# A gated linear-attention and ternary-FFN layer: the mean square of the gated output is built from squares on GpSimd, one transpose and a VectorE sum

## The reference, cut to what matters

```python
x = L0_attn_hidden_states                      # [16, 512, 256]
xn = _layernorm(x, axis=-1)
x = x + _L0_attn_ref(xn, ...) + _L0_ffn_ref(xn, ...)
...
# the end of the attention part
o = gla_chunk_scan(q * SCALE, kn, v, rt_log)
o = o + shift * residual_weight
xg = o * jax.nn.silu(final_gate)               # [B, T, 512]
rms = jax.lax.rsqrt(jnp.mean(xg * xg, axis=-1, keepdims=True) + NORM_EPS)
o = xg * rms * norm_weight
return o @ down_w.T
...
# the FFN part: three layers of width 1024
h = jax.nn.silu(_tlin(x, w1_w, w1_s)) * _tlin(x, w2_w, w2_s)
h = jax.nn.gelu(_tlin(h, h1_w, h1_s), approximate=False)
h = jax.nn.gelu(_tlin(h, h2_w, h2_s), approximate=False)
return _tlin(h, w3_w, w3_s)
```

## Time and profile before

| What | Value |
|---|---|
| Time before, median of 3 runs | 1962.21 us (1960.61 to 1963.9) |
| Time of the profiled execution | 1961.79 us |
| Its span, first to last instruction | 1960.0 us |
| Granted TensorE clock, mean | 0.999 |
| PE busy | 1941.9 us, 99% |
| DVE busy | 1581.3 us, 81% |
| ACT busy | 1266.1 us, 65% |
| POOL busy | 68.4 us, 3% |

### The profile page before, as it was taken

One profiled execution on the slowest core, in us unless ns is written; L12 is line 12 of the kernel. 1 busy time (PEld: TensorE's weight loads), 2 busy tenths in 40 slices (PEclk: granted clock), 3 DMA queues, 4 the chain that ended last, 5 costly groups with the idle time before them and its releaser, 6 DMA issues.

```text
span 1960.0 us, 46467 instructions
## 1 busy us (share of the span) xinstructions
PE 1941.9 (99%) x17284; PEld 1928.9 (98%) x17284; DVE 1581.3 (81%) x4271; ACT 1266.1 (65%) x2527; POOL 68.4 (3%) x104
## 2 busy tenths in 40 slices
PE   8999999999999999999999999999999999999998
PEld 7999999999999999999999999999999999999998
DVE  7787878878788887887878788787888878878777
ACT  5675656766566766666656566666666666667564
POOL 0000000000000000000000000000000000000000
PEclk9999999999999999999999999999999999999999
DMA  8000000000000000000000000000000000000000
GB/s 309 7 12 12 12 7 6 12 12 12 12 1 12 12 12 12 12 1 12 12 12 12 11 2 12 12 12 12 1 12 12 12 12 12 2 12 12 13 7 8
DMA packets 23538, 34.38 MB, mean 18 GB/s; under 512 B 3042, under 2 KB 19810, under 8 KB 23364
## 3 DMA queue, kind: packets, MB, share of 16 engines
q1 hardware_dynamic: 23364, 31.63, 4.9%
HBM read 23.24 MB, written 8.39 MB: 16 GB/s over the span
## 4 chain that ended last, share of the span: by engine, by line
PE 93%; issue 3%; DVE 2%; ACT 1%; SPq 1%; DMA 0%; POOLq 0%; POOL 0%; DVEq 0%; ACTq 0%
PE fb L364 63%; PE ab L364 20%; PE ab L569 2%; PE ab L602 1%; PE ab L510 1%; PE ab L434 1%; PE ab L499 1%; PE fb L650 1%; SPq L272 0%; PE ab L562 0%; PE ab L450 0%; PE ab L581 0%; PE ab L561 0%; DVE hid0l L941 0%; ACT raw L806 0%
## 5 line engine op out<-in xcount | busy, mean ns | idle before, releaser
L364 PE MATMUL fb<-hid1h,wwhole 128*128 128x256 f32 x2048 | 475.4, 280 | 1.2 <-DVE hid1l L862 1.2
L364 PE MATMUL fb<-hid1l,wwhole 128*128 128x256 f32 x2048 | 468.9, 276 | 0.0
L364 PE MATMUL fb<-hid0l,wwhole 128*128 128x256 f32 x2048 | 466.4, 276 | 0.0
L364 PE MATMUL fb<-hid0h,wwhole 128*128 128x256 f32 x2048 | 466.4, 276 | 0.0
L364 PEld LDWEIGHTS fb<-hid1h,wwhole 128*128 128x128 f32 x2048 | 384.5, 188 | 4.0 <-ACT hid1h L721 0.9
L364 PEld LDWEIGHTS fb<-hid1l,wwhole 128*128 128x128 f32 x2048 | 384.7, 188 | 0.0
L364 PEld LDWEIGHTS fb<-hid0l,wwhole 128*128 128x128 f32 x2048 | 384.5, 188 | 0.0
L364 PEld LDWEIGHTS fb<-hid0h,wwhole 128*128 128x128 f32 x2048 | 384.5, 188 | 0.0
L806 ACT ACTIVATE raw<-fb,sh_s 128x256 f32<-128x256 f32 x512 | 212.8, 467 | 128.3 <-PE fb L364 126.2
L364 PE MATMUL fb<-xntl,wwhole 128*128 128x256 f32 x1024 | 237.5, 276 | 0.0
L364 PE MATMUL fb<-xnth,wwhole 128*128 128x256 f32 x1024 | 237.5, 276 | 0.0
(11 more groups left out here) (217 smaller groups left out, 4483.2 us busy)
## 6 DMA issues: line engine op xcount, KB each, us to landing
xin<-x SPq DMA_DIRECT2D x32, 256.0 KB, 2.7
out<-xin SPq DMA_DIRECT2D x32, 256.0 KB, 2.2
stage_more<-stage_w SPq DMA_DIRECT2D x6, 512.0 KB, 7.3
sgate<-stage_w SPq DMA_DIRECT2D x4, 512.0 KB, 5.1
shift<-stage_w SPq DMA_DIRECT2D x4, 512.0 KB, 5.6
v<-stage_w SPq DMA_DIRECT2D x4, 512.0 KB, 5.7
raw<-stage_w SPq DMA_DIRECT2D x3, 512.0 KB, 6.1
mixed<-stage_w SPq DMA_DIRECT2D x3, 512.0 KB, 8.4
```

Source lines behind the costliest of these rows:

```text
L364: mm = pe.matmul(o, a, b, start=start and i == 0, stop=stop and i == len(pairs) - 1)
```

## The change

The squares leave ACT. POOL multiplies `sgate` by itself in four instructions per half, one for each pair of a chunk `c` and a block of 64 channel rows `r`: the result lies on the 64 partitions `rows(c)` of `sq`. `sq` is now [128, 8, 128], with chunk 0 on partitions 0 to 63 and chunk 1 on 64 to 127. DVE sums the eight blocks into `sqsum` [128, 128]. PE transposes `sqsum` in one pass, so that tokens lie on the partitions, and DVE sums the 64 columns of each chunk (`total`, [128, 2]) before it scales them to `msq`. In the profile's rows of a changed kernel the lines are a few numbers higher than in the kernel before.

```diff
--- before.py
+++ after.py
@@ -163,9 +163,9 @@
         tanhv = work[:, 0:NC * DI].rearrange("p (c d) -> p c d", c=NC)
         lev = work[:, 0:LEVELS * CH].rearrange("p (l t) -> p l t", l=LEVELS)
         levq = work[:, LEVELS * CH:LEVELS * (CH + UP)].rearrange("p (l t) -> p l t", l=LEVELS)
-        sq = work[:, 0:DB * N].rearrange("p (d t) -> p d t", d=DB)
+        sq = work[:, 0:NC * DB * CH].rearrange("p (d t) -> p d t", d=NC * DB)
         xn = work[:, DB * N:DB * N + NC * H].rearrange("p (c h) -> p c h", c=NC)
-        sqsum = work[:, DB * N + NC * H:]
+        sqsum = work[:, DB * N + NC * H:DB * N + NC * H + CH]
         att = sb("att", [P, NC, CH])
         atth, attl = sb("atth", [P, 2, CH], F32R), sb("attl", [P, 2, CH], F32R)
         stateh, statel = sb("stateh", [P, DI], F32R), sb("statel", [P, DI], F32R)
@@ -179,6 +179,7 @@
         msq, rms = sb("msq", [P, NC]), sb("rms", [P, NC])
         nbt, later_k, earlier_q = sb("nbt", [P, 1]), sb("later_k", [P, 1]), sb("earlier_q", [P, 1])
         qk_sum = sb("qk_sum", [P, NC])
+        total = sb("total", [P, NC])
 
         fb = [ctx.enter_context(nc.psum_tensor(f"fb{i}", [P, 512], F32)) for i in range(4)]
         ab = [ctx.enter_context(nc.psum_tensor(f"ab{i}", [P, 512], F32)) for i in range(4)]
@@ -207,7 +208,7 @@
         kd_hi, st_hi, q_hi = seq_sig("kd_hi", NC), seq_sig("st_hi", 1), seq_sig("q_hi", 1)
         st_copy, st_sum = seq_sig("st_copy", 1), seq_sig("st_sum", 1)
         gelu1_d, hid1_hi, gelu2_d, hid2_hi = sig("gelu1_d", FB), sig("hid1_hi", 4), sig("gelu2_d", FB), sig("hid2_hi", 4)
-        sq_d, xg_hi, ln_hi = sig("sq_d", 1), sig("xg_hi", 1), sig("ln_hi", 1, 1)
+        sq_d, xg_hi, ln_hi = sig("sq_d", NC * NC), sig("xg_hi", 1), sig("ln_hi", 1, 1)
 
         conv_d, l1_d, hid0_lo, shift_lo = sig("conv_d", DB * (W - 1)), sig("l1_d", FB), sig("hid0_lo", 4), sig("shift_lo", 1)
         z_lo = sig("z_lo", 1)
@@ -220,7 +221,7 @@
         qs_d, q_lo = seq_sig("qs_d", 1), seq_sig("q_lo", 1)
         ss_d, att_d, mask_d = sig("ss_d", 1), sig("att_d", LEVELS + 2), sig("mask_d", NC)
         o_d, xg_d, xg_lo = sig("o_d", 2, 2), sig("xg_d", 1), sig("xg_lo", 1)
-        sqsum_d = sig("sqsum_d", 1)
+        sqsum_d, total_d = sig("sqsum_d", 1), sig("total_d", 1)
         hid1_lo, hid2_lo = sig("hid1_lo", 4), sig("hid2_lo", 4)
         msq_d, fin_d, stat_d, var_d, xn_d, ln_lo = (sig("msq_d", 1, 1), sig("fin_d", 5, 5), sig("stat_d", 3, 3),
                                                     sig("var_d", 1, 1), sig("xn_d", 1, 1), sig("ln_lo", 1, 1))
@@ -345,6 +346,11 @@
                 pool.tensor_tensor(rkn[:], ssk[:], minus_half[:], ALU.pow).then_inc(rkn_d.sem, 1)
                 if not (last and p == HALVES - 1):
                     normalise(me)
+                pool.wait_ge(xg_d.sem, xg_d.at(me))
+                for c in range(NC):
+                    for r in range(NC):
+                        part = sgate[rows(r), :, c * CH:(c + 1) * CH]
+                        pool.tensor_tensor(sq[rows(c), r * DB:(r + 1) * DB, :], part, part, ALU.mult).then_inc(sq_d.sem, 1)
                 pool.wait_ge(msq_d.sem, msq_d.at(me))
                 pool.tensor_tensor(rms[:], msq[:], minus_half[:], ALU.pow).then_inc(rms_d.sem, 1)
 
@@ -646,9 +652,7 @@
                 mm.then_inc(dn_mm.sem, 1)
                 pe.wait_ge(sqsum_d.sem, sqsum_d.at(me))
                 pe.wait_ge(gelu2_d.sem, gelu2_d.at(me, 4))
-                for c in range(NC):
-                    mm = pe.matmul(fb[1][:, c:c + 1], sqsum[:, c * CH:(c + 1) * CH], ones[:, 0:1], start=True, stop=True)
-                mm.then_inc(rs_mm.sem, 1)
+                pe.transpose(fb[1][:, 0:P], sqsum, ident_s[:]).then_inc(rs_mm.sem, 1)
 
             def sequences(exact):
                 with rounds(pe) as seq:
@@ -837,7 +841,6 @@
                 if not (last and p == HALVES - 1):
                     ln_high(me)
 
-                act.activation(sq[:], sgate[:], ACT.Square).then_inc(sq_d.sem, 1)
                 if p == 0:
                     act.wait_ge(st_sum.sem, st_sum.at(seq))
                     act.activation(stateh[rows(0), :], state, ACT.Copy)
@@ -1176,7 +1179,10 @@
                     low(statel[rows(0), :], state, stateh[rows(0), :])
                     low(statel[rows(1), :], state, stateh[rows(0), :]).then_inc(st_lo.sem, 1)
                 dve.wait_ge(rs_mm.sem, rs_mm.at(me))
-                dve.tensor_scalar(msq[:], fb[1][:, 0:NC], 1.0 / DI, EPS, ALU.mult, ALU.add).then_inc(msq_d.sem, 1)
+                dve.tensor_reduce(total[:], fb[1][:, 0:P].rearrange("p (c k) -> p c k", c=NC), mybir.AxisListType.X,
+                                  ALU.add).then_inc(total_d.sem, 1)
+                dve.wait_ge(total_d.sem, total_d.at(me))
+                dve.tensor_scalar(msq[:], total[:], 1.0 / DI, EPS, ALU.mult, ALU.add).then_inc(msq_d.sem, 1)
                 dve.wait_ge(fin_d.sem, fin_d.at(me, 3))
                 dve.wait_ge(rms_d.sem, rms_d.at(me))
                 for c in range(NC):
```

## The result

| | Before | After |
|---|---|---|
| Median of the runs on one chip | 1962.07 us (1960.61 to 1963.9) | 1974.6 us (1973.89 to 1976.05) |
| Profiled execution; its span | 1961.79; 1960.0 us | 1973.89; 1972.1 us |
| Granted TensorE clock, mean | 0.999 | 0.999 |

The ratio is 1.0063, with a 95% interval of 1.0051 to 1.0075: the change makes the kernel 0.6% slower, 12.5 us.

What follows compares the result with a forecast made beforehand. PE, busy 99% of the span, was taken as the bound. Late sums less the saved passes, plus DVE's tail, gave 16 x (0.65 + 0.15) + 16 x 0.42 = +19.5 us, so 1981.7 us, range 1953 to 2008.

Steps and rivals of the forecast that it cites:

- Four passes against one: PE at the end of a half: one transpose for four passes saves 0.26 us a half, 8.3 us in all.
- Squares of 1.17 us: POOL: each of the four squares of 512 elements lasts 1.17 us, with bounds of 0.96 and 1.38.
- Exclusion in turns: POOL squares and DVE operations with two SBUF inputs exclude each other, whoever waits going next; a loss, chance 0.50.
- Squares done 6.94 us after `sgate`: POOL at p = 0: taking turns with DVE, the four squares end at 1059.46, `sgate` being done at 1052.52.
- PE waits 0.6 to 0.7 us for `sqsum` in nearly all halves: PE at the end of a half: the late first sum makes it wait this long in nearly all 32 halves.
- First sum keeps 2.02 us for half the outputs: DVE: the sum into `sqsum` reads as many elements and stays 2.02 us; at best it costs 1.22.
- Second sum at most 0.34, DVE's tail +0.15: DVE behind the transpose: nearest row for the second sum 0.34 us; its lateness books 0.15 us after p = 0, nothing after p = 1.
- ACT at nothing: ACT: its 1.05 us square goes, but ACT was no step of the path, so nothing was booked.
- Free engines: Rival: POOL's reads don't hold up DVE, or squares are near 0.96 us; 1954 us, chance 0.30.
- Draw: Rival: exclusion with squares near 1.02 us, or shorter first sum; wait and saving cancel, 1959 to 1966 us, chance 0.10.
- Port kept for all four squares: Rival: POOL keeps the port through all four squares, w3 waits 2.5 us; +70 us, 2032 us, chance 0.10.
- The sum's start, 1059.5 forecast: DVE, first sum at p = 0: sign in the profile, start at 1059.5 if the forecast holds, 1057.2 if not.

Runs made afterwards that it cites:

- e1: The changed kernel with POOL squaring only chunk 0 and ACT squaring chunk 1: 1959.58 us, ratio 0.9986 to the kernel before.
- e5: e1 with `xntl` written three times ahead of the first sum, so that the sum is 1.1 us later: 1969.6 us, ratio 1.0042.
- e9: The changed kernel with three sequences in a turn of the loop, leaving 4 loop edges of 14: 1973.55 us, ratio 1.0051.
- e2: The changed kernel with one product with a [128, 2] tile replacing the transpose and second sum, four squares still on POOL: 1970.09 us, ratio 1.0042.
- e8: The squares of e1 (two on POOL, two on ACT) with the [128, 2] product of e2: 1953.87 us, ratio 0.9959 to the kernel before.
- e10: e1 with the transpose made twice, giving PE as many passes as in e8: 1963.6 us, ratio 0.9996.
- e11: e8 with the second sum on DVE put back, its result unused: 1953.62 us, ratio 0.9948.
- e7: The changed kernel with POOL's squares held back until DVE has written `xntl`, except in the last half: 2085.08 us in one run.

## Why the prediction was right, and where it was not

1974.6 lies in the range, the change loses as forecast, and the first part of the mechanism is shown: POOL and DVE exclude each other in turns, make the sum late, and lateness costs 15 us (after against e1). But the path from the late sum to the time was another. In the prediction a sum costs something only if PE waits for it. With the squares and turns as measured PE never does, and the same accounting gives the gain of up to 8.3 us. So both the sign and the nearness of 12.5 us to 19.5 are in good part luck: squares that were booked too long stand where two other costs were not booked at all.

- **Four passes against one, 0.26 a half.** Right: 0.48 to 0.24 us, wherever the sum doesn't decide.
- **Squares of 1.17 us.** They last 1.04 us free and start 1.11 apart, the lower part of the bounds (0.96 to 1.38). The Trainium skill's figure (GPSIMD Engine Reference, section 3.1, Elementwise) gave an estimated 1.12 us and was nearer to the measured 1.04 than my 1.17.
- **Exclusion in turns.** Right, also as to which of DVE's operations: `partl` and the last `hid0l`. The last `hid0l` cost PE nothing: DVE was held only 0.23 and 0.29 us.
- **Squares done 6.94 us after `sgate`** (59.46 - 52.52). Measured 6.04 (1057.84 to 1063.88). Of the 0.90 between them 0.30 is the square's length and 0.68 the waits: forecast 0.51 + 1.15 + 0.60, measured 0.38 + 0.87 + 0.33, since I let POOL wait for DVE's whole occupation and the port is handed over earlier at both ends; less 0.07 that POOL started later.
- **PE waits 0.6 to 0.7 us for `sqsum` in nearly all halves. This step failed.** The sum ends 0.03 and 0.26 us before PE, not 0.64 and 0.50 after. The forecast for the boundaries, 16 x 0.65 + 16 x 0.42 = +17.1, came out at +4.6 - 4.1 = +0.5. The recorded terms are also rounded up. Unrounded, the sum ends at 1061.48 for 1060.62 and at 1120.75 for 1120.13, which less 0.26 makes +0.60 and +0.36 instead of +0.65 and +0.42, and the forecast +17.8 instead of +19.5.
- **In its place** stand two costs that I had no term for: 0.57 us at each loop edge when the sum ends 0.26 to 0.35 us ahead (e5, e9; it turns the saving there into a loss of 0.33), and the slow pace, +7.9 us, which goes with the transpose (e2, e8, e10, e11).
- **First sum keeps 2.02 us for half the outputs.** Right: 2.00.
- **Second sum at most 0.34, DVE's tail +0.15.** It lasts 0.29. In e11 it costs nothing. Only the last half, with nothing behind it, is 3.1 us longer; this was not forecast, and its cause was only read from the order of DVE's work.
- **ACT at nothing.** Right: ACT has 1% of the chain in both kernels, and taking the square from it gained nothing.
- **The rivals.** Free engines: the engines were not free, and the 1953.87 of e8, near its 1954, comes by another form (two passes, not one); with the transpose in time it is 1959.6 (e1). Draw: no. Port kept for all four squares: no, it changes hands between them.
- **Shown in the profile as announced**: one pass; squares lengthened to DVE's reads; `partl` and `hid0l` pushed. The sum's start, 1059.5 forecast, is 1063.91 - 5.34 = 1058.6 on that scale (5.34 is L655 less L650), between the two values I had named.

## What to carry to other kernels

A result that is ready just before its reader is not free: look where the program branches next, and leave the waiting engine about a microsecond of lead at a loop's back edge. When work moves to GpSimd, write out which VectorE operations with two SBUF operands run beside it and let the two take turns; if the chain is then late, give a part of the work to a ScalarE that has time to spare, as here, before giving up the change. And hold a new form on TensorE against another form of the same result in the same place, since what follows it can run at another pace.

## What the runs showed of the hardware that was not expected

- Behind a loop's back edge, the first matmul comes about 0.96 us after the end of a late DVE sum whose semaphore PE takes ahead of the edge; elsewhere it is 0.16 us. Unrolling removes it boundary by boundary (e9). What PE does in that time the profile only calls issue.
- Matmuls of 128x128 by 256 run at 0.1133 or at 0.118 us, in stretches of some 30 to 150, at the same granted clock. With a transpose ahead of `z` there are 3211 to 5177 of the slow ones, without it 1805 to 2328. What selects the pace stays open.
- POOL and DVE hand the port over 0.14 us before POOL's recorded end, and an instruction that waits for it shows the wait as its own length, not as idle time.
- Where PE waited 2.6 us for a sum in each half (e7), the granted clock fell from 2.4 to 1.2 GHz behind 16 of the waits, for 54.6 us in all, and cost an estimated 27 us on top of them. In the kernel after, whose waits at the edges are 0.5 us at most, it did not fall between the second `z` and the last.
- A DVE sum over 1024 elements with a stride lasts 2.00 us for 128 outputs and 2.02 for 256: it is paid by elements read.
